# Channel-attention stage: VectorE weighs chunk n and then subtracts chunk n+3, where it subtracted chunk n+2 and then weighed

## The chip, the cores and the metric

The kernel runs on one core of a Trainium2 chip. The metric is the device time of one execution in microseconds. A core has five engines that work side by side, each through its own list of instructions in order: TensorE (PE in the profile, its weight loads PEld), VectorE (DVE), ScalarE (ACT), GpSimd (POOL) and SyncE (SP), which issues DMAs. They are kept in step by semaphores: an instruction waits until a semaphore has reached a count.

## The reference

Four transformer layers run one after the other on 4 sequences of 512 tokens with 128 features, each an attention and a feed-forward part with a layer norm behind it. The change lies in the attention of the last layer, which attends over channels: for every token on its own, each of 16 heads has a 64 x 64 score matrix, the outer product of the token's query and key channels.

```python
def _L3_attn_ref(x, Wq, bq, Wk, bk, Wv, bv, Wo, bo):
    B, S, D = (4, 256, 128); H, C = (16, 64); HID = H * C
    b, s, _ = x.shape
    Q = (x @ Wq + bq).reshape(b, s, H, C) * (1.0 / C ** 0.5)
    K = (x @ Wk + bk).reshape(b, s, H, C)
    V = (x @ Wv + bv).reshape(b, s, H, C)
    scores = jnp.einsum('bshq,bshk->bshqk', Q, K)
    mask = jnp.triu(jnp.ones((C, C), dtype=bool), 1)
    scores = jnp.where(mask, -jnp.inf, scores)
    w = jax.nn.softmax(scores, axis=-1)
    attn = jnp.einsum('bshqk,bshk->bshq', w, V).reshape(b, s, HID)
    return attn @ Wo + bo
```

## The kernel before, in words

A loop over the 4 sequences runs all stages of one sequence. The channel stage, sixth of eight, works on 4 tiles of 128 tokens (tt = 0 to 3), one token on each partition. The score matrices of a tile are cut into 18 chunks of up to 1536 values a partition (c = 0 to 17): 6 early ones (queries of the later half, keys of the first half or so, ragged along the diagonal, some of several pieces), 8 rectangles and 4 late ones. n = 18 tt + c counts the 72 chunks of a sequence. The scores of the first 8 of the reversed query rows, the "own" ones, aren't in chunks: ScalarE makes them from the keys directly.

A chunk goes through five steps, each with a semaphore, in a ring of five buffers D3[n % 5]:

1. GpSimd multiplies queries by keys (L1319, semaphore `prod`). It waits until chunk n-5 is weighed and its denominator summed.
2. VectorE subtracts the query's maximum, read from the PSUM banks psM (L1366, `subtract`, semaphore `d`).
3. ScalarE takes the exponential in place (L1296, `e`).
4. TensorE sums the denominator with transposing matmuls (L1196, `den`).
5. VectorE multiplies by the values V into one of two buffers W3 (L1384, `weigh`, semaphore `w`), and TensorE sums these as well (L1196, `num`). Before it writes a W3 buffer, VectorE waits for the sum that last read it.

The order of the work is written out by hand, one loop over n for each engine. TensorE, in its step n, sums the denominator of chunk n, then the weighed chunk n-1, and then does what is set for that chunk: filling V (c = 3 and 17), the output projection of the tile before (c = 6, L1180, it waits for both halves of `finish`), the projections of K and Q of the next tile (c = 8 to 11, L1167 and L1168). ScalarE, in its step n, takes the exponential, moves K and Q of the next tile out of PSUM (c = 9 to 12, L1268, L1272), and from c = 2 to 14 makes 8 to 10 of the 128 own-score activations (L1286). The first of these waits for `neg`, the negated maxima NB, which VectorE writes at the end of `maxima(tt, 0)` (L1352, L1353, L1354, L1358). The own pieces are weighed by VectorE (L1390) at c = 15, 16 and 17, two each.

VectorE's loop (`channel_dve`) has, ahead of the subtraction and the weighing of a step, what is set for that chunk: `maxima(tt, 0)` at c = 1 for tiles 1 to 3, `finish(tt - 1, 0)` at 3 (a reciprocal L1400 and a multiplication L1404), `residual(tt - 1)` at 7 (L1412, it waits for the output projection), `finish(tt, 1)` at 8, `scan_keys(tt + 1)` at 12 (L1337) and `maxima(tt + 1, 1)` at 14. Tile 0 has its scan and maxima ahead of the loop. The constants:

```python
Q0_AT, MAX_0, FINISH_0, V1_AT = 0, 1, 3, 3
PROJ_AT, RESIDUAL, FINISH_1 = EARLY, EARLY + 1, EARLY + 2    # EARLY is 6
SCAN, MAX_1 = EARLY + 6, EARLY + 8
```

Of the kernel before, what the change touches and what calls it, by code (L numbers as in the profile page):

```python
# [57 lines left out]
def transformer(nc, inp, out, last_stage=8):  # L58
    ctx = ExitStack()
    with ctx:  # L60
# [1044 lines left out]
        NALL = NT * NC  # L1105
# [23 lines left out]
        def w_count(tt, item):  # L1129

            return tt * NW + in_order.index(item) + 1

        def chunk_w(n):
            return w_count(n // NC, ("chunk", n % NC))

        def of_piece(buf, piece):
            k, nk, w, at = piece
            return buf[:, at:at + nk * NH * w].rearrange("p (k q h) -> p k q h", h=NH, k=nk)

        def keys_on(a, k, nk, w):  # L1140

            v = a[:, NH * k:NH * (k + nk)].rearrange("p (k h) -> p k h", h=NH)
            return v[:, :, None, :].to_broadcast([P, nk, w, NH])

        def queries_on(a, ch, piece):

            k, nk, w, at = piece
            return a[:, NH * ch.first_query:NH * (ch.first_query + w)][:, None, :].to_broadcast([P, nk, NH * w])
# [173 lines left out]
        def channel_dve(dve):  # L1322
# [3 lines left out]
            def then(ins):  # L1326

                chain[0] += 1
                ins.then_inc(s["chain"], 1)
                dve.wait_ge(s["chain"], chain[0])  # L1330

            def scan_keys(tt):


                dve.wait_ge(s["kh"], 2 * tt + 2)
                for dst, f, op in ((PMX, first[0], ALU.max), (PMN, first[1], ALU.min)):
                    last = nc.vector.tensor_tensor_scan(dst, f[:], KH, 0.0, ALU.add, op)  # L1337
                then(last)

            def maxima(tt, half):  # L1340


                raw = tt == 0 or half == 1
                if raw:
                    dve.wait_ge(s["qk_sb"], 4 * tt + 4)
                else:
                    dve.wait_ge(s["q_ps"], tt)
                by = HD ** -0.5 if raw else 1.0
                r = slice(half * HD // 2, (half + 1) * HD // 2)
                m, low = (a.rearrange("p (c h) -> p c h", h=NH) for a in (psM[half], QN))  # L1350
                mx, mn = (a.rearrange("p (h c) -> p c h", h=NH)[:, ::-1, :][:, r, :] for a in (PMX, PMN))
                nc.vector.scalar_tensor_tensor(low, m, by, mn, ALU.mult, ALU.mult)  # L1352
                then(nc.vector.scalar_tensor_tensor(m, m, by, mx, ALU.mult, ALU.mult))  # L1353
                then(nc.vector.tensor_tensor(psM[half], psM[half], QN, ALU.max))  # L1354
                if half == 0:
                    if tt > 0:
                        dve.wait_ge(s["own"], tt * len(own))
                    nc.vector.tensor_scalar(NB, psM[0][:, 0:NH * OWN], -1.0, None, ALU.mult).then_inc(s["neg"], 1)  # L1358

            def subtract(n):  # L1360
                ch = chunks[n % NC]
                dve.wait_ge(s["prod"], n + 1)
                for piece in ch.pieces:
                    k, nk, w, at = piece
                    d = D3[n % 5][:, at:at + nk * NH * w].rearrange("p (k n) -> p k n", k=nk)
                    last = nc.vector.tensor_tensor(d, d, queries_on(psM[ch.half], ch, piece), ALU.subtract)  # L1366
                last.then_inc(s["d"], 1)

            def weigh(n):
                tt, c = n // NC, n % NC  # L1370
                for item in by_step[c]:
                    w_ = w_count(tt, item)
                    buf = W3[(w_ - 1) % 2]
                    if w_ > 2:
                        dve.wait_ge(s["num"], w_ - 2)
                    if item[0] == "chunk":
                        dve.wait_ge(s["e"], n + 1)
                        if c == 0:
                            dve.wait_ge(s["v"], 2 * tt + 1)
                        if c == LATE:  # L1380
                            dve.wait_ge(s["v"], 2 * tt + 2)
                        for piece in chunks[c].pieces:
                            k, nk, w, at = piece
                            last = nc.vector.tensor_tensor(of_piece(buf, piece), of_piece(D3[n % 5], piece),  # L1384
                                                           keys_on(psV, k, nk, w), ALU.mult)
                    else:
                        dve.wait_ge(s["own"], (tt + 1) * len(own))
                        k, nk = own_pieces[item[1]]
                        at = k * NH * OWN
                        last = nc.vector.tensor_tensor(of_piece(buf, (k, nk, OWN, 0)), of_piece(EA, (k, nk, OWN, at)),  # L1390
                                                       keys_on(psV, k, nk, OWN), ALU.mult)
                    last.then_inc(s["w"], 1)

            def finish(tt, half):

                done = tt * NC + (EARLY if half == 1 else NC)
                dve.wait_ge(s["den"], done)
                if half == 0:
                    dve.wait_ge(s["own_den"], (tt + 1) * len(own_pieces))
                then(nc.vector.reciprocal(RD, psD[half]))  # L1400
                dve.wait_ge(s["num"], chunk_w(done - 1) if half == 1 else (tt + 1) * NW)
                if tt >= 2:
                    dve.wait_ge(s["proj"], tt - 1)
                nc.vector.tensor_tensor(AT[tt % 2][:, half * HB_:(half + 1) * HB_], RD, psA[half], ALU.mult)\  # L1404
                    .then_inc(s["attn"], 1)
                dve.wait_ge(s["attn"], 2 * tt + 2 - half)

            def residual(tt):
                t = slice(tt * P, (tt + 1) * P)
                dve.wait_ge(s["proj"], tt + 1)  # L1410
                done = nrm["res"] if tt == NT - 1 else s["rT"]
                nc.vector.scalar_tensor_tensor(rT[:, t], scratch[:, 0:P], bo3[:, 0:1], xT[:, t], ALU.add, ALU.add)\  # L1412
                    .then_inc(done, 1)
# [3 lines left out]
            maxima(0, 0)  # L1417
            subtract(0)
            subtract(1)
            for n in range(NALL):  # L1420
                tt, c = n // NC, n % NC
                if tt > 0:
                    if c == MAX_0:
                        maxima(tt, 0)
                    if c == FINISH_0:
                        finish(tt - 1, 0)
                    if c == RESIDUAL:
                        residual(tt - 1)
                if c == FINISH_1:
                    finish(tt, 1)  # L1430
                if tt + 1 < NT:
                    if c == SCAN:
                        scan_keys(tt + 1)
                    if c == MAX_1:
                        maxima(tt + 1, 1)
                if n + 2 < NALL:
                    subtract(n + 2)
                weigh(n)
            finish(NT - 1, 0)
            residual(NT - 1)  # L1440

# [4 lines left out]
        with nc.Fori(0, BATCH) as b:  # L1446
            with nc.Block() as block:
# [60 lines left out]
                @block.vector  # L1508
                def _(dve):
                    attn_dve(dve)  # L1510
                    norm_dve(dve, 0, psS[0], a0["proj"], 1)
                    ffn0_dve(dve)
                    norm_dve(dve, 1, psO, f0["down"], 1, scale=s_0[:, 4 * NM:4 * NM + 1])
                    heads_dve(dve, A1)
                    norm_dve(dve, 2, psS[0], a1["proj"], 1)
                    ffn1_dve(dve)
                    norm_dve(dve, 3, psO, f1["down"], 1)
                    prune_dve(dve)
                    heads_dve(dve, A2)
                    norm_dve(dve, 4, psS[0], a2["proj"], 1, bias=bo2[:, 0:1])  # L1520
                    moe_dve(dve, m2, bg2, True)
                    norm_dve(dve, 5, psO, m2["downs"], NE * NM, twice=True)
                    channel_dve(dve)
                    norm_dve(dve, 6, None, None, 0)
                    moe_dve(dve, m3, bg3, False)
                    norm_dve(dve, 7, psO, m3["downs"], NE * NM + 1)
# [59 lines left out]
```

## Time and profile before

| | |
|---|---|
| time, median of 3 runs | 4037.76 us (4037.64 to 4039.16) |
| the profiled execution | 4039.69 us |
| its span, first to last instruction | 4037.7 us |
| mean granted TensorE clock | 0.903 of full |
| PE, PEld, DVE, ACT, POOL busy | 79, 52, 60, 51, 33% |
| L1366 subtract, DVE, x480 | 494.8 us |
| L1384 weigh, DVE, x480 | 495.4 us |
| L1296 exponential, ACT, x288 | 406.8 us |
| L1286 own scores, ACT, x2048 | 805.2 us |
| L1319 products, POOL, x480 | 1024.1 us |

Times are from the hardware profiler on one execution. A row's busy time is a sum over instructions, and idle time of an engine costs something only where that engine is what the rest waits for. The channel stage of the first sequence lies between about 523 and 954 us of the span, and those of the other sequences about 996 us apart, so it is some 1.7 ms of the 4.04. Timeline rows give start, duration, engine, line, operation, output<-input, shape and how many instructions were merged; in brackets stands the idle time of the engine before them, and what ended it.

### The profile page before, as it was taken

The page shows a single profiled execution, that of the slowest core. Times are in us where ns is not written, and L with a number is a line of the kernel's source. Part 1 is how long each engine was busy: PE and PEld are TensorE (multiplying, and loading weights), DVE is VectorE, ACT ScalarE, POOL GpSimd, SP SyncE. Part 2 cuts the span into 40 slices and gives each one's busy share as a digit, 9 for nine tenths or more (in the row PEclk, how much of TensorE's full clock was granted, in tenths as well). Part 3 has the DMA queues.
Part 4 walks back from the last instruction along what each step waited for, and adds up shares of the span by engine and source line. Part 5 has one row for each costly group of instructions (what it writes and reads, how often), then busy time and mean ns, then how long its engine had stood idle before and what let it go on. Part 6 is the DMA issues. An engine that isn't in the chain of part 4 may idle for free. (4 is left out here: it accounts for less than half of the span.)

```text
span 4037.7 us, 48798 instructions
## 1 busy us (share of the span) xinstructions
PE 3205.5 (79%) x17780; PEld 2111.1 (52%) x17780; DVE 2404.1 (60%) x4553; ACT 2069.2 (51%) x4372; POOL 1331.7 (33%) x1068
## 2 busy tenths in 40 slices
PE   4877978878787797778878779888786877888877
PEld 2434456675344446667435343666743544466673
DVE  3456378884256528888315653888731574488873
ACT  1435277773253527777225342877722543277762
POOL 0213066660021207655003120766400311166640
PEclk9989979998898898999889888999998988899998
DMA  3000100000100010000110001000010000100001
GB/s 118 1 1 1 55 1 1 1 1 21 63 1 1 1 55 1 1 1 1 55 30 1 0 2 54 1 1 1 1 55 30 1 1 15 41 1 1 1 1 57
DMA packets 69640, 68.19 MB, mean 17 GB/s; under 512 B 6491, under 2 KB 49907, under 8 KB 69254
## 3 DMA queue, kind: packets, MB, share of 16 engines
q1 hardware_dynamic: 60288, 56.15, 4.6%
q10 hardware_dynamic: 9094, 8.72, 0.7%
q8 instruction: 146, 2.39, 0.3%
q14 instruction: 112, 0.92, 0.1%
HBM read 63.81 MB, written 1.05 MB: 16 GB/s over the span
## 5 line engine op out<-in xcount | busy, mean ns | idle before, releaser
L1319 POOL TENSOR_TENSOR arena<-arena 128x1536 f32<-128x1536 f32 (+9 forms) x480 | 1024.1, 2163 | 594.9 <-DVE arena L1384 477.7
L1196 PE MATMUL psum<-ident,arena 128*128 128x128 f32 (+7 forms) x7168 | 951.9, 295 | 310.7 <-ACT arena L1296 246.3
L1196 PEld LDWEIGHTS psum<-ident,arena 128*128 128x128 f32 (+7 forms) x7168 | 865.6, 146 | 428.7 <-ACT arena L1296 261.8
L1286 ACT ACTIVATE arena<-arena 128x64 f32<-128x64 f32 (+7 forms) x2048 | 805.2, 493 | 38.9 <-DVE arena L1358 38.9
L1384 DVE TENSOR_TENSOR arena<-arena,psum 128x1536 f32<-128x1536 f32 (+9 forms) x480 | 495.4, 1068 | 115.6 <-ACT arena L1296 105.0
L1296 ACT ACTIVATE arena<-arena 128x1536 f32<-128x1536 f32 (+2 forms) x288 | 406.8, 1423 | 290.0 <-DVE arena L1366 289.7
L1366 DVE TENSOR_TENSOR arena<-arena,psum 128x1536 f32<-128x1536 f32 (+9 forms) x480 | 494.8, 1065 | 8.2 <-POOL arena L1319 6.3
L473 POOL TENSOR_TENSOR rstd<-veps,mhalf 128x4 f32<-128x4 f32 x32 | 32.4, 1011 | 1314.6 <-DVE veps L464 1314.6
L763 POOL TENSOR_SCALAR arena<-arena 128x512 f32<-128x512 f32 (+3 forms) x512 | 263.8, 532 | 590.8 <-DVE arena L735 590.8
L692 ACT ACTIVATE arena<-arena 128x512 f32<-128x512 f32 (+3 forms) x512 | 281.8, 552 | 268.9 <-DVE arena L730 268.6
L649 PE MATMUL psum<-ident,arena 128*128 128x128 f32 x1280 | 192.0, 294 | 147.5 <-ACT arena L703 88.8
L649 PEld LDWEIGHTS psum<-ident,arena 128*128 128x128 f32 x1280 | 146.5, 148 | 253.8 <-ACT arena L703 135.4
L1206 PE MATMUL psum<-ident,arena 128*128 128x128 f32 (+6 forms) x2048 | 249.1, 274 | 28.1 <-DVE arena L1390 28.1
L970 PE MATMUL psum<-arena,stream 128*128 128x512 f32 x512 | 266.2, 602 | 3.0 <-DVE arena L1091 3.0
L987 PE MATMUL psum<-arena,stream 128*128 128x512 f32 x512 | 246.6, 606 | 0.0
L1390 DVE TENSOR_TENSOR arena<-arena,psum 128x1536 f32<-128x1536 f32 (+1 forms) x96 | 150.8, 1575 | 158.5 <-PE psum L1196 155.4
L1206 PEld LDWEIGHTS psum<-ident,arena 128*128 128x128 f32 (+6 forms) x2048 | 223.5, 138 | 41.4 <-DVE arena L1390 39.6
L440 ACT ACTIVATE xT<-psum 128x512 f32<-128x512 f32 x32 | 19.1, 597 | 431.2 <-PE psum L434 431.2
L624 PE MATMUL psum<-arena 64*128 64x256 f32 (+3 forms) x1024 | 200.5, 500 | 27.4 <-DVE arena L725 22.8
L1087 DVE TENSOR_TENSOR arena<-arena,psum 128x512 f32<-128x512 f32 x128 | 88.0, 687 | 220.6 <-PE psum L987 220.6
L1019 ACT ACTIVATE arena<-psum 128x512 f32<-128x512 f32 x128 | 76.4, 597 | 274.8 <-PE psum L987 274.8
L1091 DVE TENSOR_TENSOR arena<-arena 128x512 f32<-128x512 f32 x128 | 88.6, 692 | 181.6 <-ACT arena L1021 181.6
(207 smaller groups left out, 4023.5 us busy)
## 6 DMA issues: line engine op xcount, KB each, us to landing
stream<-in_L_ffn_W SPq DMA_DIRECT2D x160, 256.0 KB, 3.1
arena<-in_L_ffn_h_w SPq DMA_DIRECT2D x8, 1024.0 KB, 8.2
arena<-in_L_ffn_w_w SPq DMA_DIRECT2D x12, 256.0 KB, 4.7
arena<-in_L_ffn_h_w ACTq DMA_DIRECT2D x2, 1024.0 KB
wa<-in_L_attn_W_attn ACTq DMA_DIRECT2D x1, 1536.0 KB
wq<-in_L_attn_Wq ACTq DMA_DIRECT2D x2, 512.0 KB
wo<-in_L_attn_Wo ACTq DMA_DIRECT2D x2, 512.0 KB
x<-in_L_attn_x SPq DMA_DIRECT2D x4, 256.0 KB, 3.7
```

The costliest lines, as they stand in the source:

```text
L649: last = nc.tensor.transpose(GX[:, half, c:c + P], two(PRG[b % 4])[:, half, c:c + P], ident[:])
L692: nc.scalar.activation(pr, pr, ACT.Exp, bias=nb[:, u:u + 1], scale=HD ** -0.5, accum_out=rsum[:, u:u + 1]).then_inc(s["probs"], 1)
L763: nc.gpsimd.tensor_scalar(pr, pr, rinv[:, u:u + 1], 1.0, ALU.mult, ALU.mult).then_inc(s["scaled"], 1)
L970: nc.tensor.matmul(psO, slot[:, 2 * HID + m * P:2 * HID + (m + 1) * P], HR[n % 3], start=n == 0, stop=top2 and n == NE * NM - 1).then_inc( ...
L987: nc.tensor.matmul(up_bank(n, j), slot[:, j * HID + m * P:j * HID + (m + 1) * P], XS[e % 2], start=True, stop=True).then_inc(s["up"], 1)
L1196: last = nc.tensor.matmul(ps[ch.half][0:rows, to:to + P], buf[:, c:c + rows], ident[:], start=first, stop=False, is_transpose=True, skip_g ...
L1206: last = nc.tensor.matmul(ps[0][0:rows, 0:P], buf[:, j * NH * OWN:j * NH * OWN + rows], ident[:], start=False, stop=k == HD - 1, is_transp ...
L1286: nc.scalar.activation(by_key[:, 0:HD - r, j], keys[:, h, 0:HD - r], ACT.Exp, bias=NB[:, j:j + 1], scale=Q3[tt % 2][:, j:j + 1]).then_inc( ...
L1296: nc.scalar.activation(D3[n % 5][:, 0:cols], D3[n % 5][:, 0:cols], ACT.Exp).then_inc(s["e"], 1)
L1319: last = nc.gpsimd.tensor_tensor(of_piece(D3[n % 5], piece), q, keys_on(K3[tt % 2], k, nk, w), ALU.mult)
L1366: last = nc.vector.tensor_tensor(d, d, queries_on(psM[ch.half], ch, piece), ALU.subtract)
L1384: last = nc.vector.tensor_tensor(of_piece(buf, piece), of_piece(D3[n % 5], piece), keys_on(psV, k, nk, w), ALU.mult)
```

## The change

In the loop over chunks, VectorE's subtraction moves behind the weighing and goes one chunk further ahead; a third subtraction stands before the loop. Nothing else is touched.

```diff
@@ -1417,6 +1417,7 @@
             maxima(0, 0)
             subtract(0)
             subtract(1)
+            subtract(2)
             for n in range(NALL):
                 tt, c = n // NC, n % NC
                 if tt > 0:
@@ -1433,9 +1434,9 @@
                         scan_keys(tt + 1)
                     if c == MAX_1:
                         maxima(tt + 1, 1)
-                if n + 2 < NALL:
-                    subtract(n + 2)
                 weigh(n)
+                if n + 3 < NALL:
+                    subtract(n + 3)
             finish(NT - 1, 0)
             residual(NT - 1)
```

## Rows read from the trace of the kernel before

**Rows 1.** The page's busy times: engine, us, share of the span, instructions.

```profile
PE 3205.5 (79%) x17780; PEld 2111.1 (52%) x17780; DVE 2404.1 (60%) x4553; ACT 2069.2 (51%) x4372; POOL 1331.7 (33%) x1068
```

**Rows 2.** Windows view, tile 1, first sequence; columns in the first row.

```profile
core 0: us, PE busy (x) PEld busy (x) DVE busy (x) ACT busy (x) POOL busy (x), PEclk, DMA share, GB/s
642.00:715.70 73.70, 56.72 (x369) 46.38 (x369) 66.34 (x58) 72.43 (x149) 49.22 (x18) 0.91 0.00 1
715.70:736.00 20.30, 18.79 (x168) 18.01 (x167) 12.50 (x13) 2.02 (x4) 9.14 (x6) 1.00 0.00 1
```

**Rows 3.** Waits, channel stage, first sequence: total us, times, longest us.

```profile
ACT arena L1296 <- DVE arena L1366: 72.5, 10, 12.6
...
DVE arena L1384 <- ACT arena L1296: 27.7, 12, 3.1
...
ACT arena L1286 <- DVE arena L1358: 9.7, 3, 3.3
```

**Rows 4.** Timeline of VectorE from the end of tile 0 into tile 1.

```profile
634.30 1.22 DVE L1390 TENSOR_TENSOR arena<-arena,psum 128x1024 f32<-128x1024 f32 x1 [1.61 <-PE psum L1196]
635.44 1.81 DVE L1366 TENSOR_TENSOR arena<-arena,psum 128x896 f32<-128x896 f32 x2
637.17 1.81 DVE L1384 TENSOR_TENSOR arena<-arena,psum 128x1024 f32<-128x1024 f32 x2
638.90 1.06 DVE L1352 SCALAR_TENSOR_TENSOR arena<-psum,arena 128x512 f32<-128x512 f32 x1
...
641.70 0.29 DVE L1358 TENSOR_SCALAR arena<-psum 128x128 f32<-128x128 f32 x1
641.91 1.81 DVE L1366 TENSOR_TENSOR arena<-arena,psum 128x832 f32<-128x832 f32 x2
643.63 1.81 DVE L1384 TENSOR_TENSOR arena<-arena,psum 128x960 f32<-128x960 f32 x2
```

**Rows 5.** Timeline of ScalarE: tile 0 (one row), tile 1, start of tile 2.

```profile
536.07 1.49 ACT L1296 ACTIVATE arena<-arena 128x1536 f32<-128x1536 f32 x1 [0.75 <-DVE arena L1366]
...
637.29 1.49 ACT L1296 ACTIVATE arena<-arena 128x1536 f32<-128x1536 f32 x1 [5.61 <-DVE arena L1366]
642.03 3.99 ACT L1286 ACTIVATE arena<-arena 128x64 f32<-128x64 f32 x10 [3.25 <-DVE arena L1358]
...
679.49 0.60 ACT L1268 ACTIVATE arena<-psum 128x512 f32<-128x512 f32 x1 [1.21 <-PE psum L1168]
...
712.03 3.71 ACT L1296 ACTIVATE arena<-arena 128x1536 f32<-128x1536 f32 x3
728.25 1.50 ACT L1296 ACTIVATE arena<-arena 128x1536 f32<-128x1536 f32 x1 [12.51 <-DVE arena L1366]
...
735.99 1.48 ACT L1296 ACTIVATE arena<-arena 128x1536 f32<-128x1536 f32 x1 [5.77 <-DVE arena L1366]
```

**Rows 6.** Line L1358 over the whole span: who waited for it (us, times).

```profile
  ACT arena L1286: 38.9, 12
```

**Rows 7.** Timeline of TensorE: two rows of tile 1, one of the second sequence.

```profile
673.14 4.41 PE L1196 MATMUL psum<-ident,arena 128*128 128x128 f32 x24 [2.35 <-ACT arena L1296]
...
713.56 1.97 PE L1196 MATMUL psum<-ident,arena 128*128 128x128 f32 x16 [1.55 <-ACT arena L1296]
...
1670.18 2.84 PE L1196 MATMUL psum<-ident,arena 128*128 128x128 f32 x24 [2.37 <-ACT arena L1296]
```

**Rows 8.** VectorE's residual in tile 1, and at the end of the stage.

```profile
667.44 0.35 DVE L1412 SCALAR_TENSOR_TENSOR rT<-psum,bo,xT 128x128 f32<-128x128 f32 x1 [1.40 <-PE psum L1180]
...
953.22 0.35 DVE L1412 SCALAR_TENSOR_TENSOR rT<-psum,bo,xT 128x128 f32<-128x128 f32 x1 [3.85 <-PE psum L1180]
```

**Rows 9.** Timeline of GpSimd: products of chunk 3, and of chunks 8 to 11, tile 1.

```profile
624.23 3.60 POOL L1319 TENSOR_TENSOR arena<-arena 128x832 f32<-128x832 f32 x2 [8.85 <-DVE arena L1384]
...
656.28 13.79 POOL L1319 TENSOR_TENSOR arena<-arena 128x1536 f32<-128x1536 f32 x4 [3.77 <-DVE arena L1384]
```

## The prediction

> **What bounds the kernel now.** I write S(c) and W(c) for the subtraction and the weighing of chunk c of a tile (0 to 17), MAX_0 for the four instructions of `maxima(tt, 0)`, and E(c) for ScalarE's exponential.
>
> I began with the busy shares of the page [rows 1]. No engine is full over the span, so the bound has to be read from the stage that changes. I took the stretches of one steady tile next, tile 1 of the first batch, in the windows view [rows 2]. From 642 to 715.7 us ScalarE is busy 72.43 of 73.70 us, while VectorE and TensorE each leave 7 us or more unused. From 715.7 to 736 TensorE is busy 18.79 of 20.30 us and ScalarE almost not at all. So a tile has two parts: one that ScalarE sets and one that TensorE sets.
>
> The waits of the stage [rows 3] say who starts each part. ScalarE's exponentials wait for a subtraction 10 times in a batch, 72.5 us. The ScalarE timeline [rows 5] places them: 12.51 us before E(0), 5.77 us before E(1) and 5.61 us before E(2) of a tile. Three such tiles make 71.7 us, and a 0.75 us wait at 536.07 in tile 0 is the tenth. After that the own-key scores wait for MAX_0: 3.25 us at 642.03, three times a batch, 12 times in the run, 38.9 us in all [rows 3, 5, 6]. From there to the last exponential (712.03 + 3.71 = 715.74) ScalarE stops once, for 1.21 us at 679.49.
>
> At the end of that run TensorE, which has idled 1.55 us, is released by E(15) at 713.56 [rows 7] and then works nearly without a pause until VectorE gets the buffers of the last own pieces (the next tile's counterpart of 634.30 [rows 4] is at 740.1). So the path is a ring: last own piece, S(2), W(0), MAX_0, ScalarE's 74 us, TensorE's end of the tile, last own piece.
>
> **The order that the edit really makes.** Written out, before is S0 S1, then H(n) S(n+2) W(n) for each n, H(n) being what stands in the step ahead of them (maxima, finish, residual, scan). After is S0 S1 S2, then H(n) W(n) S(n+3). Without H both are S0 S1 S2 W0 S3 W1 S4..., the same instructions in the same order. No weighing passes a subtraction. What changes is that S(n+2) now stands ahead of H(n). H is empty except at chunks 1 (MAX_0, tiles 1 to 3), 3 (finish, half 0), 7 (residual), 8 (finish, half 1), 12 (scan) and 14 (maxima, half 1). Nothing is added or removed, no DMA moves, and no other engine's order changes.
>
> **Chunk 1, the term that costs.** Before: W(0) 637.17, MAX_0 638.90 to 641.99, S(3) 641.91, W(1) 643.63 [rows 4]. After: S(3) starts at 638.90 and MAX_0 follows it, W(1) stays where it was. S(3) takes 643.63 - 641.91 = 1.72 us from start to start. MAX_0 ends in the negated maxima that the own-key scores wait for, so these start 1.72 us later, at 643.75 instead of 642.03. ScalarE already stood waiting for them (3.25 us), so all of it shows, and the wait becomes 4.97 us. What S(3) gives in return is worth nothing: E(3) stands behind the own scores of chunk 2 in ScalarE's queue. Queued behind the later instruction are E(3) to E(17), the eight-to-ten activations of each step, and the moves of the next Q and K. TensorE's end of the tile waits for E(15), the next tile's start for that end.
>
> Is it caught up later? ScalarE has one pause, the 1.21 us at 679.49, and that is a wait for the K projection, which TensorE issues after the transposes of chunk 8 [rows 5, 7]. Those wait for E(8), so the pause moves with ScalarE. I take the full 1.72 us. Bounds per tile: below, 1.72 - 1.21 = 0.51 us, if TensorE ran the transposes ahead of the projection faster; above, 1.82 us, the busy time of S(3).
>
> Tile 0 has its MAX_0 ahead of the loop and isn't touched. Three tiles in each of four batches: 12 x 1.72 = 20.6 us.
>
> **The other five places.** S(5), S(10), S(14) and S(16) come earlier by a whole H. ScalarE isn't waiting for any of them: all its waits for a subtraction lie at E(0), E(1), E(2) [rows 3, 5], so 0 us gained. The operations now later are the half-0 and half-1 finish, whose results TensorE wants only at chunk 6 and in the next tile, the scan and the half-1 maxima, wanted by MAX_0 and S(0) of the next tile. The weighing behind each keeps its place, since H + S is the same sum as S + H. 0 us.
>
> The residual waits 1.40 us for the output projection [rows 8], and S(9) now stands ahead of it, which would fill the wait. But the projection follows the transposes of chunk 6, which wait for E(6), now 1.72 us later; the wait comes back behind S(9), near 1.5 us. Even a full fill would only be VectorE time, and VectorE waits for ScalarE again at W(10) and W(11): 27.7 us a batch [rows 3]. 0 us.
>
> Each earlier subtraction needs GpSimd's product. The tightest is S(9): products 8 to 11 take 13.79 us from 656.28 [rows 9], so 9 is done at 663.2, and S(9) is now wanted at about 665.9. The cover is 2.7 us; if it fell, the residual would be late and nothing on the path with it. S(3)'s product was done at 627.8 [rows 9], 11 us ahead.
>
> **Sum.** The profiled execution took 4039.69 us (span 4037.7 plus 2.0 around it): 4039.69 + 20.6 = 4060.3 us. It lies 1.93 above the median of the runs, so for the median I say 4037.76 + 20.6 = 4058.4 us, 0.51% more.
>
> **The clock, row and rule.** TensorE's granted clock falls after pauses: 24 transposes take 4.41 us at 673.14, after 2.35 us idle, and 2.84 us at the same place of tile 1 in the second batch, after 2.37 us idle [rows 7], so an idle length alone doesn't decide. The change adds about 1.4 us of idle near 648, ahead of the transposes of chunk 3. The Trainium skill (TensorE: Matmul & The Clock Gate, "What's actually happening") says that idle puts the array at 1.2 GHz and sustained work brings it back to 2.4, by a monitor that runs on its own phase. By the rows the sum stays 20.6; by that rule the low spells may fall at other places, which would give the two clock rivals below.
>
> **The rivals.**
> (a) *The low spell at chunk 8 moves away.* Then the 1.21 us pause at 679.49 goes. It stands in six of the eight tiles that have it (two already run at full clock there), so 6 x 1.21 = 7.3 us back: 4051.1. For: the row of the second batch. Against: from chunk 4 on TensorE's pattern hangs on ScalarE, which moves as a whole.
> (b) *A low spell falls into the end of the tile*, where TensorE is the bound. One group of 24 costs 4.41 - 2.84 = 1.57 us, 12 x 1.57 = 18.8: 4077.2. Against: the clock is 1.00 in all of 715.7 to 736 [rows 2], and only 1.55 us idle come before it.
> (c) *The delay is absorbed*: MAX_0's result isn't what starts the tile's long part, because VectorE or the probability buffers would have held ScalarE anyway. Then 4037.8. Against: ScalarE's 3.25 us with that releaser, 12 of 12.
> (d) *The other side, faster: VectorE's own queue is the bound of the tile.* Then the delay of MAX_0 costs nothing and filling the residual's wait pays: 12 of its 16 waits [rows 8] are like the 1.40 us one (the four at the end of a batch, 3.85 us in the row, have no subtraction left to fill them), and 12 x 1.40 = 16.8 us go: 4021.0. It decides once the waits at W(10) and W(11) are under what the residual frees. Against: those waits are 5.7 us in a tile, and they grow by the 1.72.
> (e) *The edit does what its words say*, each weighing one subtraction sooner. The written-out order excludes it; it has no share of the chances.
>
> **Chances and range.** The forecast 0.78, (a) 0.06, (b) 0.05, (c) 0.07, (d) 0.04. A measurement of this kernel tells 0.2%, 8.1 us, from no change. Forecast, (a) and (b) are slower: 0.89; (c) is the same: 0.07; (d) faster: 0.04. The range goes from (a), with a little below it, 4050, to 4067, half of (b) above the forecast; the forecast's own bounds, 12 x 0.51 and 12 x 1.82, would be 4043.9 and 4059.6, but the lower one needs all twelve tiles to gain what only six can.
>
> **What would show it.** In the profile after: S(3) between W(0) and MAX_0; ScalarE's wait for L1358's negation near 4.97 us each, 59.6 in all, against 38.9; tile 0 unchanged; the period of tiles 1 and 2 up by 1.7, from 105.8 to 107.5; the three waits for S(0), S(1), S(2) unchanged; a residual wait still there behind S(9); W(10) and W(11) still waiting. I am wrong if the wait for the maxima grows and the tile period doesn't, if the 1.21 us pauses change by several us in sum, or if the end of the tile shows a clock below 1.

## The result, and the profile after

The changed kernel takes 4052.48 us (median of 7 runs, 4050.86 to 4053.69) beside 4038.36 us for the kernel before (7 runs). The ratio is 1.0034, 95% interval 1.0023 to 1.0046: 14.1 us slower. Forecast were 4058.4 us and a loss of 20.6 us. The sign, the place and the price per tile came out; a third of the loss was given back, most of it by a term that I had costed at nothing. In what follows a *pause* is an idle stretch of ScalarE ahead of a move of K or Q (L1268), and a *low spell* a stretch in which TensorE's granted clock is at the lower of its two levels, 1.2 GHz instead of 2.4.

VectorE at the start of tile 1, timeline of the kernel after, answers to [rows 4]:

```profile
634.03 1.22 DVE L1390 TENSOR_TENSOR arena<-arena,psum 128x1024 f32<-128x1024 f32 x1 [1.61 <-PE psum L1196]
635.16 1.81 DVE L1366 TENSOR_TENSOR arena<-arena,psum 128x896 f32<-128x896 f32 x2
636.89 1.81 DVE L1384 TENSOR_TENSOR arena<-arena,psum 128x1024 f32<-128x1024 f32 x2
638.62 1.81 DVE L1366 TENSOR_TENSOR arena<-arena,psum 128x832 f32<-128x832 f32 x2
640.35 1.05 DVE L1352 SCALAR_TENSOR_TENSOR arena<-psum,arena 128x512 f32<-128x512 f32 x1
...
643.11 0.29 DVE L1358 TENSOR_SCALAR arena<-psum 128x128 f32<-128x128 f32 x1
643.32 1.81 DVE L1384 TENSOR_TENSOR arena<-arena,psum 128x960 f32<-128x960 f32 x2
```

S(3) stands at 638.62 between W(0) and the maxima, and takes 1.73 us. From the last own piece to the negation it is now 643.11 - 634.03 = 9.08 us, before 641.70 - 634.30 = 7.40. W(1) keeps its distance (9.29 after, 9.33 before).

ScalarE in the same tile, answers to [rows 5]:

```profile
637.01 1.49 ACT L1296 ACTIVATE arena<-arena 128x1536 f32<-128x1536 f32 x1 [5.60 <-DVE arena L1366]
643.43 4.00 ACT L1286 ACTIVATE arena<-arena 128x64 f32<-128x64 f32 x10 [4.94 <-DVE arena L1358]
...
678.26 1.49 ACT L1296 ACTIVATE arena<-arena 128x1536 f32<-128x1536 f32 x1
679.64 0.60 ACT L1268 ACTIVATE arena<-psum 128x512 f32<-128x512 f32 x1
...
712.19 3.58 ACT L1296 ACTIVATE arena<-arena 128x1536 f32<-128x1536 f32 x3
728.41 1.49 ACT L1296 ACTIVATE arena<-arena 128x1536 f32<-128x1536 f32 x1 [12.64 <-DVE arena L1366]
```

The wait for the maxima grew from 3.25 to 4.94 us (4.97 expected). But the move of K at 679.64 has no bracket: the pause of 1.21 us is gone. The waits over the whole span, total us, times, longest, say the same of all tiles. First two lines of the kernel before:

```profile
ACT arena L1296 <- DVE arena L1366: 289.7, 40, 12.6
ACT arena L1268 <- PE psum L1168: 57.7, 22, 4.2
```

The kernel after:

```profile
ACT arena L1296 <- DVE arena L1366: 291.2, 40, 12.6
ACT arena L1286 <- DVE arena L1358: 59.3, 12, 4.9
ACT arena L1268 <- PE psum L1168: 50.2, 16, 4.2
```

The waits for a subtraction are as before, the waits for the negation rose by 20.4 us (from 38.9), and the waits for a K or Q projection are now 16, the four in each sequence that fetch tile 0's own K and Q, where the kernel before had six more. TensorE at the place of the lost pause, answers to the first row of [rows 7]:

```profile
669.42 2.84 PE L1196 MATMUL psum<-ident,arena 128*128 128x128 f32 x24 [0.56 <-ACT arena L1296]
674.62 2.84 PE L1196 MATMUL psum<-ident,arena 128*128 128x128 f32 x24 [2.36 <-ACT arena L1296]
677.30 1.02 PE L1167 MATMUL psum<-wk,xT 128*128 128x512 f32 x2
```

The transposes of chunk 8 took 2.84 us instead of 4.41, after the same idle time (2.36 us here, 2.35 before), so the projection was ready when ScalarE came for it. The granted clock of that stretch stands in the windows view, columns as in [rows 2], first the kernel before and then the kernel after:

```profile
674.00:678.00 4.00, 4.00 (x24) 3.58 (x22) 3.93 (x4) 4.00 (x9) 0.64 (x1) 0.70 0.01 2
...
674.00:678.00 4.00, 3.38 (x26) 2.88 (x26) 3.93 (x3) 4.00 (x11) 0.75 (x1) 1.00 0.00 0
```

Before, the mean is 0.70, part of the window at 1.2 GHz and part at 2.4; after, all of it is at 2.4.

**Where the time went.** The time from one negation (L1358) to the next, and from the last one to the last residual (L1412), start to start, read from VectorE's timeline, in us, one row for each sequence. The first column belongs to tile 0, the second to tile 1, and so on:

```
            before                               after
seq 0   112.63  105.78  105.84   99.90      114.35  106.23  106.09   99.06
seq 1   112.61  104.40  105.76   98.94      114.34  106.21  106.05   99.09
seq 2   112.57  105.83  105.83   99.91      114.37  106.27  106.09   99.12
seq 3   112.60  104.57  105.93   99.26      114.34  106.23  106.08   99.05
sum     450.41  420.58  423.36  398.01      457.40  424.94  424.31  396.32
```

The first column has no pause in either kernel: +6.99 us, 1.75 a tile, the pure price. In the second and third column a tile of the kernel before lasts 104.4 to 104.6 us without the pause (two tiles) and 105.8 to 105.9 with it (six). Against the tiles without it the changed kernel is 1.6 to 1.8 us longer, against those with it only 0.15 to 0.5. In the last column 1.7 us are won: the last output projection, 16 matmuls, took 3.68, 2.73, 3.68 and 3.04 us before and 2.84, 2.83, 2.89 and 2.81 after. This too is the clock. The first of the four in either kernel, and the mean granted clock in its windows row, 0.54 and 0.69:

```profile
949.42 3.68 PE L1180 MATMUL psum<-arena,wo 128*128 128x128 f32 x16 [2.72 <-DVE arena L1404]
949.42:953.10 3.68, 3.68 (x16) 3.48 (x16) 0.00 (x0) 0.00 (x0) 0.00 (x0) 0.54 0.00 0
...
951.53 2.84 PE L1180 MATMUL psum<-arena,wo 128*128 128x128 f32 x16 [2.71 <-DVE arena L1404]
951.53:954.37 2.84, 2.84 (x16) 2.54 (x16) 0.00 (x0) 0.00 (x0) 0.00 (x0) 0.69 0.00 0
```

The stage is 10.6 us longer in sum: 12 x 1.75 = 21.0 for the later negation, 1.7 back at the end, and 8.7 back in the six tiles that lost their pause. The span is 13.2 us longer (4050.9 against 4037.7); the other 2.6 us lie in stages whose code is the same, where the same stretch between two channel stages took 572.9 to 574.7 us before and 574.3 to 574.4 after.

### The profile page after: what moved, and what is told of

It is laid out like the page before. It is cut to its first block and busy times, and to the rows that moved or that the text cites. A ratio compares the mean times of both kernels' runs of the same rounds, so it can differ in the third digit from the quotient of the medians.

```text
span 4050.9 us, 48758 instructions
## 1 busy us (share of the span) xinstructions
PE 3221.6 (80%) x17780; PEld 2118.5 (52%) x17780; DVE 2400.6 (59%) x4553; ACT 2067.4 (51%) x4372; POOL 1309.2 (32%) x1068
## 5 line engine op out<-in xcount | busy, mean ns | idle before, releaser
L1196 PE MATMUL psum<-ident,arena 128*128 128x128 f32 (+7 forms) x7168 | 964.5, 297 | 310.1 <-ACT arena L1296 257.6
L1319 POOL TENSOR_TENSOR arena<-arena 128x1536 f32<-128x1536 f32 (+9 forms) x480 | 1001.6, 2114 | 630.7 <-DVE arena L1384 500.9
```

The source lines that it names most:

```text
L1196: last = nc.tensor.matmul(ps[ch.half][0:rows, to:to + P], buf[:, c:c + rows], ident[:], start=first, stop=False, is_transpose=True, skip_g ...
L1319: last = nc.gpsimd.tensor_tensor(of_piece(D3[n % 5], piece), q, keys_on(K3[tt % 2], k, nk, w), ALU.mult)
```

## The experiments

Theory A: the later negation is the whole cost, every us of it paid, and the shortfall comes from TensorE's low-clock spells, which moved off chunk 8. Theory B: the full 20.6 us are there and the other five earlier subtractions gave 6 to 7 back. Medians of the kernel before, beside each group of runs, were 4039.96, 4040.03 and 4039.66 us.

**e1_only_maxima**: from the kernel before, chunk 1 alone.

```diff
+                first_ = c == MAX_0 and tt > 0
+                if first_:
+                    subtract(n + 2)
                 if tt > 0:
                     if c == MAX_0:
                         maxima(tt, 0)
...
-                if n + 2 < NALL:
+                if n + 2 < NALL and not first_:
                     subtract(n + 2)
```

> The kernel before, with one thing of the change: at chunk 1 of tiles 1 to 3 the subtraction of chunk 3 stands ahead of the maxima; the other five places stay as before. Theory A (the delay of the negated maxima is the whole cost; the 1.2 us pauses of ScalarE before it moves K went away because TensorE's low-clock spells moved off chunk 8): the same as the changed kernel, 4050 to 4054 us, ScalarE's wait for the maxima 59 us, no pause at L1268 in tiles 1 and 2. Theory B (the full 20.6 us are there and the other five earlier subtractions gave 6 to 7 back): 4057 to 4060 us, the pauses as in the kernel before.

4054.94 us (5 runs), ratio 1.0037 (1.0024 to 1.0051): the changed kernel's time within the uncertainty, from one moved subtraction. Its waits over the span:

```profile
ACT arena L1286 <- DVE arena L1358: 59.3, 12, 4.9
ACT arena L1268 <- PE psum L1168: 53.6, 20, 4.2
```

The move of the first half of K has no pause in any tile; four shorter ones, of 0.87 us, stand at the move of the second half of Q, where the transposes of chunk 11, ahead of its projection, took 4.5 us; their tiles last 107.0 us instead of 106.1. The range by theory A was missed by 0.9 us. The four stages are 6.5 us longer than in the changed kernel, 3.4 in the columns that hold these pauses and 3.1 at the last projections (3.57 to 3.69 us each), and the stretches between the stages are 4.4 us shorter; what sets these no run tells.

**e2_all_but_maxima**: the changed kernel without chunk 1.

```diff
                     if c == MAX_0:
                         maxima(tt, 0)
+                        subtract(n + 2)
...
                 weigh(n)
-                if n + 3 < NALL:
+                held = n + 1 > NC and (n + 1) % NC == MAX_0
+                if n + 3 < NALL and not held:
                     subtract(n + 3)
```

> The changed kernel, with the maxima of chunk 1 put back ahead of the subtraction of chunk 3; the other five subtractions stay ahead of finish, residual, scan and the second maxima. Theory A: no difference from the kernel before, 4036 to 4041 us, ScalarE's wait for the maxima 39 us, pauses at L1268 as before. Theory B: 4030 to 4033 us.

4039.34 us (11 runs), ratio 0.9998 (0.9989 to 1.0007). The wait for the negation is back at 38.9 us. So the five other moves cost nothing and bring nothing that shows (the interval is 4.4 us less to 2.8 more); theory B, which has 6 to 7 us less, falls. In this trace four of the eight tiles have the pause, and their periods are again 105.8 to 105.9 with it and 104.4 to 104.6 without.

**e3_maxima_at_0**: the changed kernel, maxima at chunk 0.

```diff
-        Q0_AT, MAX_0, FINISH_0, V1_AT = 0, 1, 3, 3
+        Q0_AT, MAX_0, FINISH_0, V1_AT = 0, 0, 3, 3
```

> The changed kernel with the maxima set for chunk 0 instead of 1: VectorE does S(2), maxima, W(0), S(3). The negated maxima come one weighing (1.73 us) earlier than in the kernel before and 3.45 earlier than in the changed one. Theory A: 12 x 1.73 = 20.8 us under the kernel before, 4017.6 us, with up to 7.3 us less or 2.4 us more by the pauses; ScalarE's wait for the maxima 12 x 1.5 = 18 us. Rival C (weighing chunk 0 late holds TensorE and the ring of buffers, so that an earlier start of the own scores gives nothing): 4035 to 4045 us.

4014.2 us (5 runs), ratio 0.9935 (0.9921 to 0.9949): 25.8 us under the kernel before, 5 us more than the 20.8 of the negation alone and inside the range that the forecast gave for the pauses. VectorE, and ScalarE's first own scores, in its timeline:

```profile
635.97 1.81 DVE L1366 TENSOR_TENSOR arena<-arena,psum 128x896 f32<-128x896 f32 x2
637.70 1.05 DVE L1352 SCALAR_TENSOR_TENSOR arena<-psum,arena 128x512 f32<-128x512 f32 x1
...
640.46 0.29 DVE L1358 TENSOR_SCALAR arena<-psum 128x128 f32<-128x128 f32 x1
640.67 1.81 DVE L1384 TENSOR_TENSOR arena<-arena,psum 128x1024 f32<-128x1024 f32 x2
```

```profile
637.82 1.49 ACT L1296 ACTIVATE arena<-arena 128x1536 f32<-128x1536 f32 x1 [5.60 <-DVE arena L1366]
640.79 3.98 ACT L1286 ACTIVATE arena<-arena 128x64 f32<-128x64 f32 x10 [1.49 <-DVE arena L1358]
```

W(0), now behind the maxima, starts 3.0 us later than before, counted from S(2). TensorE waits 3.80 us for it (at 642.53) and GpSimd 7.18 (at 642.56), before 0.84 and 4.20, but neither wait is on the path: tile 0 is 1.75 us shorter and the tiles behind it, with and without a pause, 1.6 to 1.9, like for like, which is the 1.73 us of the earlier negation. Rival C falls. The first step fell from 112.6 to 110.86 us, the others to 102.6 to 102.8 without a pause and 104.1 with one.

**e4_k_projection_first**: the kernel before, in TensorE's loop.

```diff
                 if n < NALL:
+                    if c == EARLY + 2 and tt + 1 < NT:
+                        fill_qk(pe, tt + 1, 0)
                     if tt > 0 and c == 0:
...
-                if c in FILL_AT and tt + 1 < NT:
+                if c in FILL_AT and FILL_AT[c] > 0 and tt + 1 < NT:
```

> The kernel before, with TensorE's first projection of K for the next tile put ahead of the transposes of chunk 8 instead of behind them, so that ScalarE's move of K can't wait for those transposes at a low clock. Theory A: the six pauses of 1.2 us go and the time falls by 5 to 8 us, 4030 to 4034 us; by tiles, those two that had no pause don't change. Rival D (the pauses aren't on the path; ScalarE would wait elsewhere for as long): 4037 to 4040 us.

4029.58 us (8 runs), ratio 0.9975 (0.9964 to 0.9985), 10.4 us less. TensorE at chunk 8, the projection now ahead:

```profile
670.94 1.02 PE L1167 MATMUL psum<-wk,xT 128*128 128x512 f32 x2
671.89 1.12 PE L1168 MATMUL psum<-bqkv,ones 1*128 1x512 f32 x2
673.48 2.84 PE L1196 MATMUL psum<-ident,arena 128*128 128x128 f32 x24 [0.46 <-ACT arena L1298]
```

The pause is on the path: seven of the eight periods are 104.3 to 104.5 us, and the eighth, 105.84, has one of 1.34 us at the first Q projection, whose transposes ran at the low clock. Rival D falls. But the transposes of chunk 8 ran at full clock in all eight tiles (2.84 us), so the trace doesn't tell whether the new order or a spell that moved took the pauses away. The gain is larger than the pauses alone (7.2 us by the periods); 2.6 us more lie between the last negation and the end of the stage, where the last projections took 3.39, 2.05, 2.05 and 2.98 us (before 3.68, 2.73, 3.68 and 3.04).

**e5_after_k_first**: the same edit in the changed kernel.

> The changed kernel, with the first K projection put ahead of the transposes of chunk 8 as in e4. In the changed kernel no tile has the pause, in the kernel before six of eight have it. Theory A (pauses and the delay of the maxima are separate terms): nothing is left to gain here, 4050 to 4054 us, and the difference to e4 is the full price of the maxima, 20 to 25 us, where changed minus before was 14. Theory B (the change's shortfall has to do with the earlier subtractions): the difference to e4 stays near 14.

4052.32 us (7 runs), ratio 1.003 (1.0019 to 1.0042): nothing gained where there was no pause. Freed of pauses on both sides, the change costs 4052.32 - 4029.58 = 22.7 us (two groups of runs, whose kernels before differ by 0.1). That is the 20.6 of the forecast and 2 us more. By the traces the periods of tiles 0 to 2 grow by 19.8 us, with one pause left on either side, and 2.2 us lie in the last column, where the last projections of e5 took 12.65 us in sum and those of e4 10.47.

**e6_two_subtracts_first**: the kernel before, with two subtractions ahead.

```diff
+                if c == MAX_0 and tt > 0:
+                    subtract(n + 2)
+                    subtract(n + 3)
+                    ahead = {n + 2, n + 3}
                 if tt > 0:
                     if c == MAX_0:
                         maxima(tt, 0)
...
-                if n + 2 < NALL:
+                if n + 2 < NALL and n + 2 not in ahead:
```

> The kernel before, with the subtractions of chunks 3 and 4 both ahead of the maxima in tiles 1 to 3. The negated maxima come 1.72 + 1.79 = 3.5 us later a tile than before. Theory A (every us of that delay is paid, with no floor): 1.79 x 12 = 21.5 us over the changed kernel, 4074 us, up to 8 more if the low-clock spells bring the pauses back; ScalarE's wait for the maxima 80.8 us. Rival (the first 1.72 us hit something that the next don't, such as a wait for a particular buffer): 4052 to 4062 us.

4068.62 us (5 runs), ratio 1.007 (1.0056 to 1.0084). The wait in tile 1 and the total:

```profile
645.88 4.00 ACT L1286 ACTIVATE arena<-arena 128x64 f32<-128x64 f32 x10 [6.67 <-DVE arena L1358]
...
ACT arena L1286 <- DVE arena L1358: 80.1, 12, 6.7
```

The wait is the forecast 80 us and the four stages are 21.2 us longer than in the changed kernel, as theory A has it (21.5). The first column, which has no pause, grows by another 1.70 us a tile. Four pauses of 0.57 to 0.89 us are there too, at the move of the second half of Q, and the last projections took 2.8 us less. The time is only 16.1 us longer (14.5 if each is taken from its own kernel before), outside both ranges: the three stretches between channel stages took 572.3 to 572.8 us instead of 574.3 to 574.4, 5.3 us less in sum, in unchanged code. So the delay is paid in the stage as theory A has it. Why the unchanged code was faster is not tested.

**e7_maxima_0_k_first**: e3 and e4 together.

> e3 and e4 together: the changed kernel with the maxima at chunk 0 (S(2), maxima, W(0), S(3)) and the first K projection ahead of the transposes of chunk 8. e3's profile still had one pause of 1.33 us in each sequence. Theory A: the terms add, 4 x 1.4 = 5.6 us under e3, 4008.6 us. Rival (the pause moves to the second K projection or to Q's, at the same place of the low-clock spells): 4013 to 4016 us.

4011.35 us (5 runs), ratio 0.993 (0.9916 to 0.9943): 28.7 us under the kernel before, the fastest of the study. Its four stages are 5.7 us shorter than e3's (1662.9 against 1668.6), as added terms would have it, and the profiled executions are 6.4 us apart (4017.05 and 4010.61). But the first is the slowest of its five and the second the fastest of its five. By the medians, each against its own kernel before, e7 gains only 2.9 us on e3, between the two forecasts (4008.6, and 4013 to 4016), so that the terms add up is shown for the stage of these two executions and not for the median. The one pause left, 0.86 us in one tile, stands at the move of the second half of Q.

**e8_maxima_before_s2**: the kernel before, with only the constant MAX_0 set to 0.

> The kernel before with the maxima set for chunk 0, so that VectorE does maxima, S(2), W(0), S(3), W(1). The negated maxima come 3.46 us earlier than before, but E(2), which stands ahead of the own scores on ScalarE, comes 3.0 us later, so the own scores start when E(2) ends, about 0.3 us earlier than before. Theory A with the queue: 0 to 4 us under the kernel before, 4035 to 4040 us. Rival (the time of the negated maxima alone decides): 12 x 3.46 = 41.5 us under it, 3998 us.

4039.85 us (11 runs), ratio 0.9999 (0.999 to 1.0008). ScalarE at the start of tile 1:

```profile
640.85 1.48 ACT L1296 ACTIVATE arena<-arena 128x1536 f32<-128x1536 f32 x1 [8.58 <-DVE arena L1366]
642.24 3.99 ACT L1286 ACTIVATE arena<-arena 128x64 f32<-128x64 f32 x10
```

The negation is done at 639.1 and nobody waits for it; but E(2) stands ahead of the own scores and its subtraction is 3 us late. What counts is the later of the two, S(2) with E(2) and the maxima; the rival, by which the negation alone decides, falls. So the gain of e3 needs both, the maxima at chunk 0 and S(2) ahead of them. Periods are 105.5 us, 0.3 less than before, with the pause in all eight tiles.

**e9_before_again, e10_v_fill_early, e11_after_v_fill_early**: where do the pauses come from? The first is the kernel before once more; the others take away TensorE's idle time at the head of a tile, in the kernel before and in the changed one.

```diff
-        Q0_AT, MAX_0, FINISH_0, V1_AT = 0, 1, 3, 3
+        Q0_AT, MAX_0, FINISH_0, V1_AT = 0, 1, 3, 1
```

> The kernel before, unchanged, to see a second trace of it. Theory A (a pause at the move of K is there only where TensorE's clock is low in the transposes of chunk 8, and that hangs on where the low spells fall in an execution): the count of pauses may differ from the six of eight of the first trace, and each pause goes with transposes of 4.2 us or more; tiles without it have a period of 104.4 us, tiles with it 105.8. Rival (the pause has a fixed place in the order of the work): six of eight again, in the same tiles.

> The kernel before, with TensorE's filling of the second half of V set for chunk 1 instead of 3, where TensorE stands idle 3.40 us; nothing of VectorE's or ScalarE's order changes. Theory A: the idle time before chunk 2 shrinks to 1.3 us, the low-clock spell behind it (6.47 us for 42 transposes) goes or moves, and with it the later spells; the count of pauses changes from six of eight, 1.4 us each: 4030 to 4042 us. Rival (the 2.35 us of idle right ahead of chunk 8 set the spell there): six to eight pauses, 4038 to 4042 us.

> The same edit in the changed kernel, which has no pause. Theory A: pauses may come back, at 1.4 us each: 4052 to 4063 us. Rival: no pause, 4050 to 4054 us. ScalarE's wait for the maxima stays 59 us by both.

e9 took 4042.86 us (one run), and again six of eight tiles paused. Tile 2 paused in all four sequences, as in the first trace; tile 1 in sequences 0 and 3, where the first trace has 0 and 2. So place and execution both have a part. e10 took 4039.93 us (10 runs), ratio 0.9998 (0.9988 to 1.0008), five of eight paused (tile 2 of all four sequences, tile 1 of one). e11 took 4051.84 us (9 runs), ratio 1.0032 (1.0022 to 1.0042), no pause. TensorE at the head of tile 1 in e10, and the pause further on:

```profile
642.53 1.02 PE L1173 MATMUL psum<-wv,xT 128*128 128x512 f32 x2
...
647.61 1.75 PE L1196 MATMUL psum<-ident,arena 128*128 128x128 f32 x14 [1.33 <-DVE arena L1384]
```

```profile
681.64 0.60 ACT L1268 ACTIVATE arena<-psum 128x512 f32<-128x512 f32 x1 [1.20 <-PE psum L1168]
```

The idle time at the head and the low spell behind it went as expected in this tile, and the pause stayed, so the early idle time doesn't place the later spells. This guess of mine fell. e11 shows no pause where I expected some to come back, as its rival said.

What holds over all of it: in the ten traces in which the transposes of chunk 8 stand right ahead of the first K projection, tiles 1 and 2 of four sequences each, 80 tiles, the move of K paused in 33, and in just those 33 the 24 transposes took 4.30 to 4.51 us; in the other 47 they took 2.84. One row of either kind from e9, sequence 0 and sequence 1, after the same idle time:

```profile
675.12 4.42 PE L1196 MATMUL psum<-ident,arena 128*128 128x128 f32 x24 [2.36 <-ACT arena L1296]
...
1672.19 2.84 PE L1196 MATMUL psum<-ident,arena 128*128 128x128 f32 x24 [2.37 <-ACT arena L1296]
```

In the three kernels with the change's chunk 1 (after, e1, e11) the count is 0 of 24; in the three with the order of before at chunk 1 and an unmoved projection (two traces of the kernel before, e2, e10) it is 21 of 32: tile 2 in 16 of 16, tile 1 in 5 of 16.

The tile 1 cases aren't loose either. 69.2 us after tile 0's negation stand 24 transposes whose length tells where the last low spell of tile 0 fell. In these four traces of the old order they took 4.31 to 4.33 us in five sequences, and in just those five tile 1 paused; in the other eleven they took 2.84 us, or 4.14 to 4.16, or ran on into the next 24 (8.4 us for the 48), and it didn't. So where a spell falls in a tile goes with where the last one fell in the tile before. In the three kernels with the change's chunk 1 the same 24 took 4.30 to 4.32 us in seven sequences, and tile 1 paused in none. From the same start, then, the new order leads the spells elsewhere.

## Why the prediction was right, and what it mis-sized

- *The bound, a ring through ScalarE's long part*: right. e3 shortens and e1 and e6 lengthen every tile by the time that the negation is moved.
- *The order really made, and that only chunk 1 matters*: right. e1 is the change's cost, e2 is nothing.
- *The price, 12 x 1.72 us*: right. 1.75 us in the tiles without a pause on either side, 20.4 us more waiting for the negation, 22.7 us between e5 and e4 (2.2 of it in the last projections).
- *"The pause moves with ScalarE", costed at nothing*: the step that was mis-sized. The argument was that the projection hangs on E(8), so it moves along. That is so, but the pause hung on the transposes between them being at the low clock, and in the changed kernel they never were. Six pauses went. Two of the signs that the prediction itself set failed by this: tiles 1 and 2 last 106.1 to 106.3 us and not 107.5, and the pauses changed by 7.5 us in sum, which it had named as a sign of being wrong. This was rival (a), to which I had given 0.06, with 7.3 us; by the periods a pause is worth 1.3 to 1.45 us and six of them 8 to 9, more than the 1.21 us of its row. Its 4051.1 us was the nearest of all the numbers to the measured 4052.5, which lies 5.9 us below the forecast. So the forecast was right on the negation. That the time came so near owes something to luck, since no working said how many pauses would go.
- *Rivals (b), (c), (d)*: the end of tiles 0 to 2 stayed at full clock (1.00 from 715.7 to 736 us in the trace after too), no delay was absorbed (e1, e6), and VectorE wasn't the bound (e2). The residual's wait was still there behind S(9), 1.26 us in tile 1 and 2.92 in tiles 2 and 3 (rows L1412 of the kernel after), where about 1.5 was worked out; the earlier S(9) brought and cost nothing that e2 shows. The idle time ahead of the transposes of chunk 3 came to 0.58 us at 648.86, where 1.4 was worked out.
- *Not foreseen*: 1.7 us less in the last projections and 2.6 us more in stages with unchanged code.

On the clock, the Trainium skill (TensorE: Matmul & The Clock Gate, "What's actually happening") says that the activity monitor's phase is its own and isn't set by the kernel's start. The traces fit this: with the same work and the same idle time right ahead (2.36 and 2.37 us in e9), one tile is low and another isn't, and two executions of one kernel differ in which (tile 1 of sequences 2 and 3). They don't show the monitor itself. What no run here settles is how the changed order keeps the spell off chunk 8 every time. In its trace a low group stands at chunk 6 in four of the eight tiles (4.2 us, 21.1 us after the negation) and, in all eight, the next at chunk 10; I tried one cause, the idle time at the head, and it was not that.

## What to carry to other kernels

Write out the order that an edit of a software pipeline really makes: here "weigh, then subtract the next but two" was the old order, except that one subtraction slipped ahead of the one short helper whose result another engine stood waiting for. Put the instructions that start an engine's long, unbroken part directly behind what that engine needs first, and everything else after them; the same edit with the helper one step earlier turned a loss of 0.34% into a gain of 0.65%. And a short wait that shows in some tiles and not in others of the same code is not a fixed part of the schedule: ask what differs between the tiles before carrying it over.

## What the runs showed of the hardware that wasn't expected

The granted clock of 24 transposes, which weren't on the path themselves at full clock, decided 1.3 to 1.4 us a tile, by making one projection late for ScalarE. Over the stretches between two channel stages, the same code took between 571.7 us (e2) and 575.1 us (e3) in different traces, so comparisons of a few us between kernels that only differ elsewhere need the stage's own marks beside the total.
